# Local attention layers: the product with the values in tiles of 32 keys, in two phases

## The reference

```python
for i in range(DEPTH):                                   # DEPTH = 6
    x = attn_layer(shift_tokens(x), Wqkv[i], q_scale[i], k_scale[i], Wo[i]) + x
    x = ffn_layer(shift_tokens(x), ln_g[i], ln_b[i], W1[i], b1[i], W2[i], b2[i]) + x

def attn_layer(x, Wqkv, qs, ksc, Wo):                    # HEADS = 16, DIM_HEAD = 64
    q, k, v = split into heads(x @ Wqkv)
    q = l2norm(q) * qs;  k = l2norm(k) * ksc
    q, k = rotary(q, scale), rotary(k, 1 / scale)
    return local_attention(q, k, v) @ Wo

def local_attention(q, k, v):                            # WINDOW = 32, 8 windows
    bk2, bv2 = look(bk), look(bv)                        # window before and own window: 64 keys
    mask = (it < jb) | (it > jb + w) | (jb == -1)        # jb == -1: before the first window
    sim = einsum('bhwie,bhwje->bhwij', bq, bk2) * 8
    attn = softmax(where(mask, -max, sim), -1)
    return einsum('bhwij,bhwje->bhwie', attn, bv2)

def ffn_layer(x, g, bln, W1, b1, W2, b2):                # DIM_INNER = 341
    xn = (x - mean) / sqrt(var + 1e-05) * g + bln
    a, gate = split(xn @ W1 + b1)
    return a * gelu(gate) @ W2 + b2
```

## Time and profile before

| | |
|---|---|
| median of three runs | 2818.03 us |
| lowest and highest | 2814.33 and 2821.95 us |
| span of the profiled execution | 2820.1 us |
| PE busy in the span | 2481.4 us (88%) |
| weight loads on PE busy | 1693.3 us (60%) |
| DVE busy | 2006.5 us (71%) |
| ACT busy | 1754.3 us (62%) |
| POOL busy | 1467.4 us (52%) |

### The profile page before, as it was taken

How to read it: one execution, slowest core, us unless ns; L and a number is a source line. 1 busy time by engine, 2 the same in 40 slices (tenths; PEclk the granted TensorE clock), 3 DMA queues, 4 the chain that set the end, 5 groups by cost and what they waited for, 6 DMA issues and landing times. The chain is left out here.

```text
span 2820.1 us, 93390 instructions
## 1 busy us (share of the span) xinstructions
PE 2481.4 (88%) x35216; PEld 1693.3 (60%) x35244; DVE 2006.5 (71%) x3066; ACT 1754.3 (62%) x3659; POOL 1467.4 (52%) x1068
## 2 busy tenths in 40 slices
PE   7999858985647777589999999999999999999994
PEld 4777546664433344246666666666666666766663
DVE  5888653224218888768887888887888887888883
ACT  4666523333216777457777777777777777777773
POOL 2444223222124444366666666666666666666660
PEclk9999969998768999889999999999999999999997
DMA  9100016860410000111111112111211111121110
GB/s 333 35 0 0 20 34 169 233 189 25 132 38 1 0 0 0 53 28 27 26 48 41 39 26 56 34 26 41 58 30 26 48 41 28 37 56 34 26 26 29
DMA packets 124765, 147.61 MB, mean 52 GB/s; under 512 B 12240, under 2 KB 111632, under 8 KB 120336
## 3 DMA queue, kind: packets, MB, share of 16 engines
q1 hardware_dynamic: 120592, 138.22, 18.3%
q0 software_dynamic: 4096, 8.40, 1.0%
HBM read 75.27 MB, written 27.26 MB: 36 GB/s over the span
## 5 line engine op out<-in xcount | busy, mean ns | idle before, releaser
L2372 POOL TENSOR_TENSOR c<-a,bq 128x1024 f32<-128x1024 f32 x192 | 455.0, 2370 | 144.0 <-DVE bq L2437 129.6
L2033 PE MATMUL ps<-wqk,xs 128*128 128x512 f32 x768 | 372.3, 607 | 22.5 <-POOL xs L2365 17.8
L2382 POOL TENSOR_TENSOR qn<-c,ss 128x1024 f32<-128x1024 f32 x192 | 365.2, 1902 | 28.4 <-issue 3.4
L2436 DVE TENSOR_TENSOR a<-ps,tab 128x512 f32<-128x512 f32 x384 | 263.0, 685 | 83.4 <-ACT sq L2209 80.1
L2209 ACT ACTIVATE sq<-ps 128x512 f32<-128x512 f32 x384 | 224.5, 597 | 95.4 <-PE ps L2033 61.2
L2437 DVE TENSOR_TENSOR bq<-ps,tab 128x512 f32<-128x512 f32 x384 | 261.3, 681 | 0.0
L1425 POOL TENSOR_TENSOR hC<-hs,Cs 128x1024 f32<-128x1024 f32 x64 | 150.2, 2352 | 177.6 <-ACT Cs L1570 91.2
L2390 POOL TENSOR_TENSOR z<-z,sm 128x1024 f32<-128x1024 f32 x96 | 182.6, 1902 | 109.8 <-DVE sm L2465 99.1
L2444 DVE TENSOR_REDUCE ss<-sq 128x16 f32<-128x1024 f32 x192 | 230.3, 1199 | 3.9 <-POOL qn L2382 2.4
L2044 PEld LDWEIGHTS ps<-ident,qn 128*128 128x128 f32 x1536 | 173.1, 141 | 78.3 <-POOL qn L2382 40.6
L2033 PEld LDWEIGHTS ps<-wqk,xs 128*128 128x128 f32 x768 | 133.6, 192 | 128.6 <-issue 118.8
(11 more groups left out here) (313 smaller groups left out, 5759.3 us busy)
## 6 DMA issues: line engine op xcount, KB each, us to landing
Ve<-Vo SPq DMA_DIRECT2D x96, 256.0 KB, 4.3
Ve<-Vo SPq DMA_DIRECT2D x96, 192.0 KB, 4.4
win_rows<-rows_q SPq DMA_DIRECT2D x24, 256.0 KB, 3.3
outs_q<-win_out SPq DMA_DIRECT2D x24, 256.0 KB, 2.9
wqk<-in_wqkv SPq DMA_DIRECT2D x6, 1024.0 KB, 5.2
leaves<-in_f_w SPq DMA_DIRECT2D x9, 576.0 KB, 4.3
leaves<-in_q_w SPq DMA_DIRECT2D x1, 4608.0 KB, 18.8
leaves<-in_k_w SPq DMA_DIRECT2D x1, 4608.0 KB, 22.5
```

The lines of the kernel that those rows point to most:

```text
L2033: nc.tensor.matmul(jobs.out(n), xs[:, t * 128:(t + 1) * 128], wqk[:, (2 * y + s) * 512:(2 * y + s + 1) * 512], start=True, stop=True).then ...
L2372: nc.gpsimd.tensor_tensor(f(c), f(a), f(bq), ALU.add).then_inc(c_ready.sem, 1)
L2382: nc.gpsimd.tensor_tensor(qn[:, t, y, :, :, :].rearrange("p h s e -> p h (s e)"), c[:, y, :, :, :].rearrange("p h s e -> p h (s e)"), spre ...
L2436: nc.vector.tensor_tensor(a[:, y, :, s, :], Zs, spread(table(0, s), H1), ALU.mult)
```

## The change

- The value product takes 32 keys at a time. A product has 32 keys by 64 columns and the 64 queries that see those keys (32 at the end of the sequence). There are no more shifted copies: `Vw` holds each group of 64 tokens on two row groups of 32, once for the even and once for the odd heads. The results of even and odd key windows overlap in PSUM, so they are added up in two phases: each phase has 64 products, and in each phase each of the four row groups writes a bank of its own (`O00`, `O01`, `O10`, `O11`); in the second phase the two row groups of a pair swap banks.
- `begin_values` runs the first phase after `S0` at the end of iteration `m + 1`. `end_values` runs the second one in the iteration after, behind `Z00`. ACT's `take_outputs` copies all four banks there, and `WO` comes behind `Z01` and `T11`.
- The values are projected with four full products of 512 columns (`project_values`, one per bank). ACT writes `Vs`; four transfers re-lay it into `Vw`. SP waits for the second phase (`filled` of the four banks) before it issues them.
- The masks are eight products per block, in the tiles of the scores. The first window's mask comes out of other rows (`first_b`) of the same products, and the second mask product is gone. `scores` waits for `T{t}0` too.
- New banks, and a new order on PE, ACT and DVE; on POOL `unit(0, 0)` moves ahead of `rotary_sum(0, 1)`. DVE's `rotary(0, 1)` is cut in two halves.

```diff
-        Vo, Ve = (sb(n, [128, NG, H1 // 2, E1]) for n in ("Vo3", "Ve3"))
+        Vs, Vw = sb("Vs3", [128, NT, 2, H1 // 2 * E1]), sb("Vw3", [128, NG, H1 // 2, E1])
-        pT = sb("pT3", [128, NT, H1 // 2, 128])
+        pT = sb("pT3", [128, H1 // 2, T])
@@ order
-        order = (two(FRONT, "Z00", 0, 7) + [(LATE, "WO", 4)] + two(MID, "T10", 1, 0) + two(FRONT, "Z01", 5, 3) + two(MID, "T11", 0, 4)
-                 + two(MID, "P0", 7, 1) + [(LATE, "mean", 6)] + two(MID, "S1", 0, 5) + two(FRONT, "Z11", 2, 7) + [(LATE, "var", 4)]
-                 + two(MID, "O0", 6, 3) + two(FRONT, "T00", 1, 0) + [(FRONT, "V0", 6), (FRONT, "V1", 4)] + two(FRONT, "T01", 5, 7)
-                 + two(FRONT, "Z10", 3, 2) + two(FRONT, "S0", 5, 0) + two(MID, "P1", 7, 1)
-                 + [(LATE, "F0", 6), (LATE, "F1", 3), (LATE, "F2", 4), (FRONT, "V2", 1), (FRONT, "V3", 2)] + two(MID, "O1", 5, 0)
-                 + [(LATE, "OUT2", 3)])
+        order = (two(FRONT, "Z00", 2, 0) + two(FRONT, "Z01", 5, 4) + two(MID, "T11", 7, 3) + [(LATE, "WO", 1)] + two(MID, "T10", 3, 2)
+                 + two(MID, "P0", 7, 0) + [(LATE, "mean", 1)] + two(MID, "S1", 6, 3) + two(FRONT, "T00", 5, 4) + [(LATE, "var", 0), (FRONT, "V0", 1)]
+                 + two(FRONT, "Z11", 5, 7) + [(FRONT, "V1", 3), (FRONT, "V2", 6)] + two(FRONT, "T01", 0, 2) + two(FRONT, "Z10", 3, 6)
+                 + [(FRONT, "V3", 2)] + two(MID, "P1", 4, 0) + [(LATE, "F0", 5), (LATE, "F1", 7), (LATE, "F2", 1)] + two(FRONT, "S0", 0, 4)
+                 + [(MID, f"O{j}{g}", b) for j, g, b in ((0, 0, 6), (0, 1, 7), (1, 0, 3), (1, 1, 1))] + [(LATE, "OUT2", 5)])
@@ SP, share_values
+                    for n in VALUES:
+                        sp.wait_ge(*jobs.filled(it, n))
+                        sp.sem_inc(sp_steps, 1)
                     sp.wait_ge(V_ready.sem, V_ready.at(it, 1))
-                    for p in (0, 64):
-                        sp.dma_start(Ve[p:p + W, :, :, :], Vo[p:p + W, :, :, :]).then_inc(shared, 16)
-                        sp.dma_start(Ve[p + W:p + 2 * W, 1:NG, :, :], Vo[p + W:p + 2 * W, 0:NG - 1, :, :]).then_inc(shared, 16)
+                    for j in range(2):
+                        for c in range(2):
+                            sp.dma_start(Vw[64 * j:64 * j + 64, c::2, :, :].rearrange("p c m e -> p c (m e)"),
+                                         Vs[64 * c:64 * c + 64, :, j, :]).then_inc(shared, 16)
@@ PE, scores
-                    for j in range(2):
-                        r = slice(64 * j, 64 * j + 64)
-                        nc.tensor.matmul(jobs.out(f"S{t}.{j}"), ident_b[r, :], wmask_b[r, :, :], start=True, stop=False, tile_position=(64 * j, 0))
-                    for j in range(2 if t == 0 else 0):
-                        ...
+                    for w in range(4):
+                        rows = first_b if t == 0 and w == 0 else ident_b[:, w * W:(w + 1) * W]
+                        for j in range(2):
+                            r = slice(64 * j, 64 * j + 64)
+                            nc.tensor.matmul(jobs.out(f"S{t}.{j}")[w * W:(w + 1) * W, :], rows[r, :], wmask_b[r, :, :],
+                                             start=True, stop=False, tile_position=(64 * j, w * W))
@@ PE, values projected and multiplied
-                        for p in (0, 64):
-                            last = nc.tensor.matmul(jobs.out(n)[p:p + 64, :], xs[:, g * 64:(g + 1) * 64],
-                                                    wv[:, p * 8:p * 8 + 512], start=True, stop=True, tile_position=(0, p))
+                    nc.tensor.matmul(jobs.out(n), xs[:, t * 128:(t + 1) * 128], wv[:, j * 512:(j + 1) * 512],
+                                     start=True, stop=True).then_inc(jobs.sem_filled(n), 1)
+                def values(m, second):
+                    pe.sem_inc(pe_steps, 1)
+                    for i, a, half in itertools.product(range(4), range(2), range(2)):
+                        for j, e in itertools.product(range(2), range(2)):
+                            g = 1 - e if second else e
+                            h, v, r, n = 4 * g + 2 * a + half, 2 * i + e, 64 * j + 32 * e, f"O{j}{g}"
+                            q0, qw = v * W, min(2 * W, T - v * W)
+                            last = nc.tensor.matmul(jobs.out(n)[64 * half:64 * half + 64, a * T + q0:a * T + q0 + qw], Vw[r:r + W, v // 2, h, :],
+                                                    pT[r:r + W, h, q0:q0 + qw], start=(not second and i == 0 and a == 0),
+                                                    stop=(second and i == 3 and a == 1), tile_position=(r, 64 * half), skip_group_check=True)
+                            if second and (i, a, half) == (3, 1, 1):
+                                last.then_inc(jobs.sem_filled(n), 1)
@@ PE, body (new order)
+   Z00; end_values(n); Z01; T11; WO; T10; P0; mean; S1; T00; var; V0; Z11; V1; V2; T01; Z10; V3; P1; F0-F2; S0; begin_values(m); OUT2
@@ ACT, take_outputs
-                    for j in range(2):
-                        name = f"O{t}.{j}"
-                        act.wait_ge(*jobs.filled(it, name))
-                        nc.scalar.activation(oT[:, 4 * j:4 * j + 4, t * 128:(t + 1) * 128], pairs_view(jobs.out(name)), ACT.Copy)\
+                    for i, name in enumerate(VALUES):
+                        act.wait_ge(*jobs.filled(it - 1, name))
+                        nc.scalar.activation(oT[:, 2 * i:2 * i + 2, :].rearrange("p c q -> p (c q)"), jobs.out(name), ACT.Copy)\
@@ ACT, body (new order)
+   squares(00); take_outputs; roots(00); squares(01); turned(11); turned(10); roots(01); take_weights(0); square_centered; turned(00)
+   root_variance; exps(1); V0; squares(11); V1; V2; turned(01); affine; squares(10); roots(11); take_weights(1); gelus; V3; roots(10); exps(0)
@@ DVE, body (new order)
+   square_sums(00); rotary(00); half of rotary(01); add_attention; square_sums(01); other half; center; less_maximum(1); by_root; sums(1)
+   rotary(11); square_sums(11); square_sums(10); rotary(10); gated; less_maximum(0); add_hidden; sums(0)
```

More of the change, by code:

```diff
@@ L1939, in local1 @@
         shared = core.sem("l1f_values_shared")
-        pe_steps, pool_steps = core.sem("l1f_pe_steps"), core.sem("l1f_pool_steps")
+        pe_steps, pool_steps, sp_steps = (core.sem(f"l1f_{e}_steps") for e in ("pe", "pool", "sp"))
+        values_begun = core.sem("l1f_values_begun")
+        VALUES = [f"O{j}{g}" for j in range(2) for g in range(2)]
         SHARES = 4 * 16
@@ L2093, in turn_weights @@
                         last.then_inc(jobs.sem_filled(n), 1)
-                def values(it, m, t):
-                    pe.wait_ge(shared, m * SHARES + SHARES)
-                    for j in range(2):
-                        pe.wait_ge(*jobs.taken(it, f"P{t}.{j}"))
-                        pe.wait_ge(*jobs.free(it, f"O{t}.{j}"))
-                    pe.sem_inc(pe_steps, 1)
-                    for i, w in [(i, w) for m4 in range(0, H1, 4) for w in range(4) for i in range(m4, m4 + 4)]:
-                        j, h = i % 2, i // 2
-                        p, n = 64 * j, f"O{t}.{j}"
-                        V = Ve if w % 2 == 0 else Vo
-                        half, at = 64 * (h % 2), (h // 2) * 128 + w * W
-                        last = nc.tensor.matmul(jobs.out(n)[half:half + 64, at:at + W], V[p:p + 64, 2 * t + w // 2, h, :],
-                                                pT[p:p + 64, t, h, w * W:(w + 1) * W], start=True, stop=True, tile_position=(p, half))
-                        if i >= H1 - 2 and w == 3:
-                            last.then_inc(jobs.sem_filled(n), 1)
+                def values(m, second):
+                    pe.sem_inc(pe_steps, 1)
+                    for i, a, half in itertools.product(range(4), range(2), range(2)):
[8 more added lines that the diff above has]
+                                last.then_inc(jobs.sem_filled(n), 1)
+                    if not second:
+                        last.then_inc(values_begun, 1)
@@ new lines, in begin_values, with end_values @@
+                def begin_values(it, m):
+                    pe.wait_ge(shared, m * SHARES + SHARES)
+                    for t in range(NT):
+                        for j in range(2):
+                            pe.wait_ge(*jobs.taken(it, f"P{t}.{j}"))
+                    for n in VALUES:
+                        pe.wait_ge(*jobs.free(it, n))
+                    values(m, False)
+                def end_values(m):
+                    pe.wait_ge(values_begun, m + 1)
+                    values(m, True)
@@ L2172, in body @@
                     do(front, pair("Z00"), project, 0, 0)
+                    if late:
+                        end_values(n)
+                    do(front, pair("Z01"), project, 0, 1)
+                    do(mid, pair("T11"), turn, m, 1, 1)
                     do(late, ("WO",), outputs, n)
                     do(mid, pair("T10"), turn, m, 1, 0)
-                    do(front, pair("Z01"), project, 0, 1)
```

(8 more changed lines are left out.)

132 lines of the change are left out of this document (59 added, 73 removed).

## The result

| | before | after |
|---|---|---|
| median of four runs on one chip | 2819.99 us | 2773.43 us |
| lowest and highest | 2814.33 and 2825.91 | 2766.78 and 2777.25 |
| span of the profiled execution | 2820.1 | 2768.3 |
| PE busy | 2481.4 (88%) | 2393.4 (86%) |
| DVE, ACT, POOL busy | 2006.5, 1754.3, 1467.4 | 1983.0, 1761.3, 1476.9 |

A forecast was written before the change was run, and what follows sets the result against it. Bound by PE's issue order: PE's terms take the period from 32.48 to 30.39 us, a wait makes it 30.7; over 46 iterations 82 us, less 2 at the end, is 80 off 2818.03: 2738 us, range 2706 to 2796.

The forecast's parts named there:

- Bound by PE's issue order: Local layers: PE is busy for all 32.48 us of a period, so what it need not issue comes off.
- Value product, 4.00 to 2.84: Two blocks of 128 passes on PE, each 1.42 us like the scores' block: -1.16 us a period, bounds 0 and -2.00.
- Rivals A: Value product: only four tiles work at once, phases stay at 2.00 us each; period 31.9, 2793 us; chance 0.12.
- C: Value product: row groups don't overlap, 4.0 us a phase; period 35.9, 2975 us, slower; chance 0.12.
- Value projection -0.29: Values on PE: four full products instead of eight half-width ones, 3.73 to 3.44 us a period; bounds -0.3 and 0.
- Masks -0.24: Mask products on PE: 0.25 us for each block instead of 0.31 and 0.43; bounds 0.21 and 0.31 each.
- Neighbours -0.40: PE's order: boundaries between full-array and tiled stages, about 0.1 us each, fall from 13 to 7: -0.40 us a period.
- Copies of O, transfers, tight banks: Hand-overs to PE: ACT's four copies (2.18 us) are covered, transfers land in 4.3 us, tight banks hold; no cost.
- The wait before the first phase: PE waits about 0.3 us there for DVE's gating to empty bank 1, making the period 30.7 us.
- The ring that did not bind: WO, DVE, first phase, OUT2, Z00, second phase, Z01, T11, WO: sets the period at 30.7 instead of 30.4 us.
- by_root 1.85: DVE's by_root, from 16.0, is held up by POOL's unit(0, 1) and ends at 17.85: +0.55 us on DVE's chain.
- The end, +2: Kernel's end: second phase, copies and WO follow OUT2 with no other work: about +2 us once, bounds 0 and +5.

The follow-up runs named there:

- masks_old: The changed kernel with the old masks: two products over all columns and the extra one for the first window; period 31.46 us, 2786.28 us in one run.
- v_halves: The changed kernel with the values projected in eight half-width products again; period 32.08 us, 2810.18 us in one run.
- half_queries: The changed kernel with 32 queries in each value product, the next window's left out; period 30.94 us, 2761.94 us in one run.
- quarter: The changed kernel with value products of 32 queries and 32 weight columns, ACT copying only the rows made; period 30.52 us, 2748.10 us in one run.
- dve_plus: The changed kernel with one more, unused reduction on DVE between WO and gating; period 31.09 us, 2766.75 us in one run.
- adjacent: The changed kernel with the edits of fewer_waits and v3_cover, and the second phase directly behind the first, ahead of OUT2; period 31.16 us, 2779.58 us.
- fewer_waits: The changed kernel with four of PE's nine waits before the first phase dropped and a fifth moved ahead of S0; period 30.78 us, 2758.02 us.
- v3_cover: The changed kernel with product V3 moved from behind Z10 to between S0 and the first phase; period 30.74 us, 2751.17 us.

## Why the prediction was right, and where its sizes were off

The time lay in its range, 35 us above the forecast, and the range was wide (2706 to 2796). By its own steps:

- **Bound by PE's issue order: right.** masks_old, v_halves and half_queries each change PE's passes alone. Their stages grow or shrink by 0.34, 0.95 and 0.18 in all, and the period moves by 0.35, 0.97 and 0.16.
- **Value product, 4.00 to 2.84: right in kind, mis-sized.** It is 3.00. The scores' block was the right row (11.1 ns a pass), and the new one runs at 11.7. That is +0.16. Rivals A (2.00 a phase) and C (over 2.3) are out: measured are 11.7, 11.1 and, in quarter, 9.6 ns a pass. The floor of about 25 ns between starts that the Trainium skill, TensorE: Matmul & The Clock Gate, Part 1 ("Wait — 56ns, not 53.3ns?"), states, and that the prediction set beside C, thus does not hold for these passes in tiles.
- **Value projection -0.29: right** in place (0.86 a product). v_halves shows it together with its boundaries as 0.97, where the prediction had them as two terms.
- **Masks -0.24: right**, 0.23 each instead of 0.25.
- **Neighbours -0.40: right but for one missed.** Z00 got its 0.10 for the phase behind it; Z01, with the phase ahead of it, needed 0.10 too. PE's passes sum to 30.53 rather than 30.39.
- **Copies of O, transfers, tight banks: right.** Four copies take 2.07, from 2008.54, and WO starts at 2011.12 unhindered. Transfers land in 4.0, and no row waits for them.
- **The wait before the first phase: right place, wrong cause, too small.** 0.3 for DVE's gating was expected, and it is 0.58 for PE's own queue of waits. DVE's chain from WO to the end of gating took 17.47 (2014.96 to 2032.43), not 18.14, and did not bind. The change part by part named SP's queue, ACT's and DVE's, and not that of the engine that gained waits. That is the step that failed. The ring that did not bind had lifted the forecast period from 30.39 to 30.7, nearer to the 31.10 measured: that much of the forecast was luck.
- **by_root 1.85: wrong.** It takes 0.42:

```profile
L2488 DVE TENSOR_TENSOR cent<-cent,lrs x48: 414/416/426, 1273.3 to 2740.8; 128x256 f32<-128x256 f32 x48
```

  It starts in the same moment as POOL's product (2021.20), and it is POOL that takes longer, 2.18 instead of the 1.90 of the earlier trace rows. That DVE came first is read from the lengths alone. The rule of the Trainium skill, SBUF — State Buffer, "Who interferes with whom", which the prediction drew on, agrees in kind, with the sides exchanged: the later one has to wait. POOL's product is 0.28 longer, though, less than the 0.42 that DVE's lasts. The prediction's error was who is later, and the two starts that it laid out lay 0.3 us apart. It made no difference: DVE then stands 0.79 for ACT's exponentials, and the ring over bank 1 does not bind (dve_plus).
- **The end, +2: too small**, 7.3. WO comes 6.2 later after OUT2 than before, with 2.45 of waiting for ACT, some 2.3 in gaps before and within the second phase, and the slower clock from 2723.28 on. The prediction priced it with rows of the steady loop. It put the waits for instructions at nothing: without gaps within phases, in masks_old and v_halves, the end is 2.9 and 3.4 longer than before, inside its bounds of 0 and 5.

The forecast was 80 for the two profiled executions, which differ by 51.8. So the missing 28 us: in the 43 steady steps 0.14 a step for PE's passes and 0.27 for the wait, 6 and 11.4; the first four steps 4.6; the start of the stage 0.8; the end 5.3. In the first steps the gaps within blocks of scores and values sum to 5.4 us in after and 1.2 in before, and most of the 4.6 can be put down to them, though no run shows it. The other 7 of the 35 are no part of the kernels' difference: the profiled execution of before took 3.9 more than the median that the forecast started from, and that of after 3.3 less than its own median.

**Open.** No edit tested that the gaps within phases are waits for instructions; where in the code a block ends was not varied on purpose. It is not known why T11 and WO grew in adjacent, nor whether boundaries are all of V3's 0.20.

## What to carry to other kernels

Where an engine is bound by its issue order, count its waits as instructions: a wait that is already met still costs some 0.1 us here, unless a long instruction stands ahead of it in the queue. Price tiled and full-array stages with their boundaries, some 0.1 us each here, and group them so that there are few. And look at which of two stages is hidden when a step is put at the end of a loop, since the last iteration has no other work beside it. Price what runs outside the loop with rows from there, for dense blocks of short passes can stand still there for 1 to 2 us, as they never do in the steady loop.

## What was unexpected of the hardware

- An instruction of PE's queue that waits for what is already met, or counts up, costs about 0.1 us. Eight of them behind passes of 11 ns show as 0.58 us (after), five as 0.25 (fewer_waits), eight behind the product V3 as no idle time (v3_cover).
- PE stands still within dense blocks of short passes that run outside the steady loop, 0.3 to 2.7 us at a time, and goes on 2.2 to 3.0 us after a packet of 16 KB of instructions has started (66 gaps, in all the kernels here).
- The cost of a pass with 32 rows hardly depends on its arithmetic: 11.7 ns with 64 columns and 64 queries, 11.0 with half the queries, 9.6 with half of both.
- A phase that waits by semaphore for the last pass of the one directly before it leaves PE idle for 0.17 us (adjacent).
- by_root on DVE is 1.37 long when POOL's product is already running, and 0.42 when both start together; POOL's product takes 1.90 in the first case and 2.18 in the second.
